# Graph attention on one core: two PSUM banks for the picked destinations, running maxima in SBUF, and another order in the drain

## The chip, the cores and the metric

One core of one Trainium2 chip runs the whole program. The metric is the time of one execution in microseconds (us), lower is better. TensorE (PE) does matmuls and transposes, VectorE (DVE) and ScalarE (ACT) work element by element, GpSimd (POOL) here does nothing but issue indirect DMAs (gathers and one scatter, by indices that lie in SBUF), and SyncE (SP) issues ordinary DMAs. PSUM has 8 banks of 128 x 512 f32.

## The reference

A graph has 12500 nodes with 128 features and 212500 edges, sorted by destination. For each edge three logits per head (8 heads of 16) are formed, each gets a softmax over the edges of one destination, and the sum of the three softmaxes weights the destination's value vector:

```python
h = relu(layernorm(x))
q = h @ Wq.T + bq;  k = edge_attr @ Wk.T + bk;  v = h @ Wv.T + bv
in_m   = sum(q[src] * k, per head)
out_m  = sum(q[dst] * k, per head)
diag_m = sum(q[src] * q[dst], per head)
score = (segment_softmax(in_m / 4, dst) + segment_softmax(out_m / 4, dst)
         + segment_softmax(diag_m / 4, dst)) * edge_weight ** lam
h = segment_sum(score * v[dst], dst)
out = x + leaky_relu(h @ Wo.T + bo, 0.1)
```

## The kernel before, in words

**Node pass.** `node_pass` normalises x and writes the tables q_tab (queries of all nodes) and v_tab to HBM. POOL meanwhile gathers 77 of 99 rows of destination numbers (`fetch_rows`, L141), which DVE compares and counts (`count`, L129 and L133) to find the last edge of each node.

**Edge pass.** `edge_pass` goes over 104 units of 16 tiles of 128 edges, each unit in 4 groups of 4 tiles. Per group: POOL gathers 4 tiles of source queries from q_tab (`fetch_sources`, L150, 16 gathers a unit, 1664 in all) into a ring `qsrc` of 8 groups; SP loads windows of q_tab around the group's destinations (L744); DVE makes a one-hot mask from the destination numbers (`pick_mask`, L1004); PE picks the destinations' queries by a matmul of window and mask into `qd_ps` (`pick`, L822), multiplies the edge features by Wk into `k_ps` (`keys`, L811) and transposes the gathered sources into `qs_ps` (`turn`, L831). ACT copies `qd_ps` and `k_ps` to `kq` (`take_qd` L897, `take_k` L891), DVE forms the three products (`products`, L1014 and L1018), and PE sums them over the heads into `lg_ps` (`sums_of_heads`, L802).

Per unit, one unit later: DVE scans the logits for running maxima per segment into `max_ps` (`running_max`, L1029), ACT copies them to `sums` (`take_max`, L909), DVE forms the differences (L1035, L1037, L1040), ACT takes their exponentials (`exps`, L913 to `terms`, and L914, the decay factors, over `max_ps`), and DVE weights the terms (`running_sums`, L1045) and scans twice for running sums (L1050). Two units later PE transposes maxima and sums into `t_ps` (`turn_sums`, L842), ACT copies them to `rows` (`take_rows`, L921), and `finish_unit` stores them to `state` in HBM (L931).

All orders are written out by hand in each engine's `unit(h, q)`; there is no scheduler. PE asks in `pick` that ACT has copied every earlier pick, since `qd_ps` is one bank:

```python
need(pe, qd_copied, n)
```

DVE calls `running_max` after the products of a unit's group 0, and `running_sums` after those of group 3, in the last unit ahead of those of group 3. ACT calls `exps` at group 2.

**Drain.** What follows POOL's last source gather is called the drain: the last logits, maxima and sums, their store, the join of the 128 partitions' ends (`join_ends`, `join_fix`), a gather of one row each of `state` (L777), its repaired version scattered back (L782), and the last destination rows (`fetch_rows` for blocks 7 and 8, 11 gathers each; block 7 stands ahead of the wait for the stores, `rows_out`, and block 8 between L777 and L782).

**Out pass.** POOL gathers 98 times 128 rows of `state` (`fetch_results`, L159), and the rest turns them into the output behind it.

Of the kernel before, what the change touches and what calls it, by code (L numbers as in the profile page):

```python
# [24 lines left out]
P = 128  # L25
# [19 lines left out]
A = 3  # L45
# [544 lines left out]
def edge_pass(nc, env):  # L590
# [8 lines left out]
    with ExitStack() as ctx:  # L599
# [14 lines left out]
        prod = sb("prod", [P, 2, A, GRP * P])  # L614
        terms = sb("terms", [P, 2, A, W1])
        sums = sb("sums", [P, 2, 3, A, W1])
        diffs = sb("diffs", [P, 2, A, W1])
# [25 lines left out]
        k_ps = psum("k_ps", [P, 2, GRP * P])  # L643
        qd_ps = psum("qd_ps", [P, GRP * P])
        qs_ps = psum("qs_ps", [P, 2, GRP * P])
        max_ps = psum("max_ps", [P, A, W1])
        lg_ps = psum("lg_ps", [P, A, W1])
# [111 lines left out]
        @block.gpsimd  # L759
        def _(pool):  # L760
            def unit(h, q):
                u = QUAD * h + q
                pool.wait_ge(idx_in[q], 16 * (h + 1))
                for g in range(NG):
                    need(pool, qs_turned, NG * u + g - RING + 1)
                    pool.sem_inc(pool_turns, 1)
                    fetch_sources(pool, q, g)

            for b in range(2):
                pool.wait_ge(env["q_out"][b], 16 * (NSTEP // 2))  # L770
            pool.wait_ge(env["zeros_out"], 16)
            over_units(pool, unit)

            fetch_rows(pool, NEARLY, tile_i)
            for b in range(2):
                pool.wait_ge(rows_out[b], 16 * (NCOL // 2))
            pool.indirect_dma_start(out=fix[:, :, :].rearrange("p k c -> p (k c)"), out_offset=None, in_=state,  # L777
                                    in_offset=bass.IndirectOffsetOnAxis(ap=fix_i[:, 0:1], axis=0)
                                    ).then_inc(fix_in, 16)
            fetch_rows(pool, NB - 1, tile_i)  # L780
            pool.wait_ge(fixed_ready, 1)
            pool.indirect_dma_start(out=state, out_offset=bass.IndirectOffsetOnAxis(ap=fix_i[:, 0:1], axis=0),  # L782
                                    in_=fixed[:, :, :].rearrange("p k c -> p (k c)"), in_offset=None
                                    ).then_inc(fix_out, 16)
            pool.wait_ge(edge_step, 20)
            pool.wait_ge(env["rows_used"], NEARLY)
            pool.wait_ge(fix_out, 16)
            pool.sem_inc(pool_turns, 1)
            for k in range(RST):
                fetch_results(pool, k)  # L790

        @block.tensor
        def _(pe):
# [20 lines left out]
            def pick(h, q, m):  # L814
                n = NG * (QUAD * h + q) + m
                r, w = slot(q, m)
                pe.wait_ge(window_in[r], 16 * GRP * (2 * h + w + 1))
                need(pe, qd_copied, n)
                pe.wait_ge(onehot_ready, n + 1)
                for j in range(GRP):  # L820
                    at = slice(j * P, (j + 1) * P)
                    t = nc.tensor.matmul(qd_ps[:, at], window[:, r, j, :], onehot[:, m % 2, at], start=True, stop=True)  # L822
                t.then_inc(qd_ready, 1)
# [22 lines left out]
            def unit(h, q):  # L846
                v = scanned(h, q)
                for g in range(NG):
                    if exists(h, q, g + 1):
                        pick(h, q, g + 1)  # L850
                        keys(h, q, g + 1)
                    if is_last(h, q) and g == NG - 1:
                        for k in range(3):
                            turn_sums(NCOL - 2, 0, k)
                    if exists(h, q, g - 1) and g != 1:
# [5 lines left out]
                    if g == 1:  # L861
                        sums_of_heads(h, q, g - 1)

            env["nodes_done"](pe)
# [3 lines left out]
            over_units(pe, unit)  # L868
            sums_of_heads(NQUAD, 0, -1)
            for k in range(3):  # L870
                turn_sums(NCOL - 1, 1, k)
# [5 lines left out]
            for k in range(2):  # L877
                t = nc.tensor.transpose(qd_ps[0:CH, k * P:(k + 1) * P], pens[:, k, :], ident[:, :])
            t.then_inc(ends_turned, 1)
# [6 lines left out]
        def _(act):  # L886
# [7 lines left out]
            def take_qd(h, q, m):  # L894
                n = NG * (QUAD * h + q) + m
                act.wait_ge(qd_ready, n + 1)
                nc.scalar.copy(kq[:, m % 2, 1, :], qd_ps[:, :]).then_inc(qd_copied, 1)  # L897

# [8 lines left out]
            def take_max(v, b):  # L907
                act.wait_ge(max_ready, v + 1)
                nc.scalar.copy(sums[:, b, 0, :, :], max_ps[:, :, :]).then_inc(max_copied, 1)  # L909

            def exps(v):
                act.wait_ge(diffs_ready, v + 1)
                nc.scalar.activation(terms[:, 0, :, 1:W1], diffs[:, 1, :, 1:W1], ACT.Exp, scale=SCALE)  # L913
                nc.scalar.activation(max_ps[:, :, :], diffs[:, 0, :, :], ACT.Exp, scale=SCALE).then_inc(exps_ready, 1)  # L914

# [29 lines left out]
            def unit(h, q):  # L945
                v = scanned(h, q)
                for g in range(NG):
# [12 lines left out]
                    if g == 2 and done:  # L960
                        finish_unit(v - 1, q % 2)
                    if g == 2 and v is not None:
                        exps(v)
                    if is_last(h, q) and g == NG - 1:
                        take_rows(NCOL - 2, 0, 0)
                        take_rows(NCOL - 2, 0, 1)
                        finish_unit(NCOL - 2, 0)

# [7 lines left out]
            over_units(act, unit)  # L976
            seed(NCOL - 1)
            take_max(NCOL - 1, 1)
            take_rows(NCOL - 1, 1, 0)
            exps(NCOL - 1)  # L980
# [11 lines left out]
        def _(dve):  # L992
# [29 lines left out]
            def running_max(v, p, n, b):  # L1022
# [5 lines left out]
                pen = pa_sb[:, p, 0:A, :]  # L1028
                nc.vector.tensor_tensor_scan(max_ps[:, :, :].rearrange("p a i -> p (a i)"),  # L1029
                                             pen.rearrange("p a i -> p (a i)"),  # L1030
# [5 lines left out]
                                        ).then_inc(logits_used, 1)  # L1036
                nc.vector.tensor_tensor(shifted[:, :, :], max_ps[:, :, 0:P],  # L1037
                                        pen[:, :, 1:W1], ALU.add).then_inc(shift_ready, 1)
                dve.wait_ge(shift_ready, v + 1)
                nc.vector.tensor_tensor(diffs[:, 0, :, 1:W1], shifted[:, :, :], max_ps[:, :, 1:W1], ALU.subtract  # L1040
                                        ).then_inc(diffs_ready, 1)

            def running_sums(v, p, b):
# [5 lines left out]
                for k in (1, 2):  # L1049
                    s = nc.vector.tensor_tensor_scan(sums[:, b, k, :, :].rearrange("p a i -> p (a i)"),  # L1050
                                                     max_ps[:, :, :].rearrange("p a i -> p (a i)"),
                                                     terms[:, k - 1, :, :].rearrange("p a i -> p (a i)"), 0.0,
# [3 lines left out]
            def unit(h, q):  # L1056
# [3 lines left out]
                for g in range(NG):  # L1060
                    if is_last(h, q) and g == 3:
                        running_sums(v, p, 1 - q % 2)
# [13 lines left out]
            def join_ends():  # L1076

                dve.wait_ge(ends_turned, 1)
                nc.vector.tensor_copy(ends[:, 0:3, :], k_ps[0:CH, 0, 0:3 * P].rearrange("p (k n) -> p k n", k=3))
                nc.vector.tensor_copy(ends[:, 3:5, :], qd_ps[0:CH, 0:2 * P].rearrange("p (k n) -> p k n", k=2)  # L1080
                                      ).then_inc(join_step, 1)
# [388 lines left out]
```

## Time and profile before

| | us |
|---|---|
| median of 3 runs | 2389.36 (2387.71 to 2393.61) |
| the profiled execution | 2390.79 |
| span of its records | 2389.0 |
| PE busy | 1799.0 (75%) |
| DVE busy | 1749.4 (73%) |
| ACT busy | 933.9 (39%) |
| POOL busy | 1775.7 (74%) |

The profiled execution's own time is 1.8 us above its span and 1.4 us above the median. Times within the trace count from the start of the span. An engine's busy time leaves out register, branch, semaphore and DMA-issuing instructions on the queues, but POOL's indirect DMAs are counted, since POOL works out their descriptors. An idle time is put down to what ended last before it ended; "issue" is idle time in which the engine waited for nothing that the profile shows.

### The profile page before, as it was taken

What the parts mean: (1) busy time and instruction counts of PE and PEld (TensorE: products, weight loads), DVE (VectorE), ACT (ScalarE), POOL (GpSimd) and SP (SyncE); (2) the same over time, 40 slices, a digit from 0 to 9 for tenths busy, and PEclk for the clock granted to TensorE, in tenths of its full rate; (3) what the DMA queues carried; (4) which work ended last, traced back from release to release, by engine and by line L of the source; (5) the groups of instructions that cost most, each with busy time, mean ns of one, the idle gap of its engine ahead of it and who ended that gap; (6) DMA issues with size and microseconds to landing.
All of it is one profiled execution on the core that took longest, in us unless ns stands there. A gap on an engine that the chain in (4) does not pass through costs nothing.

```text
span 2389.0 us, 44129 instructions
## 1 busy us (share of the span) xinstructions
PE 1799.0 (75%) x10768; PEld 1101.8 (46%) x10768; DVE 1749.4 (73%) x2904; ACT 933.9 (39%) x1931; POOL 1775.7 (74%) x1869
## 2 busy tenths in 40 slices
PE   5557888887778777777777777878878788877277
PEld 4424444444444444444444444444444444444155
DVE  6749887777777777777777777777777777777456
ACT  5413444443434444344344443443434334434112
POOL 5777777777777777777777777777777777777575
PEclk9868998888989889889898898898888888899567
DMA  7797887777777777777777777777777777774345
GB/s 259 227 297 217 247 260 230 224 224 221 231 229 225 218 233 227 231 219 222 224 233 223 231 220 221 233 222 223 232 220 233 224 224 229 226 218 123 125 146 169
DMA packets 440885, 527.91 MB, mean 221 GB/s; under 512 B 87325, under 2 KB 306721, under 8 KB 440850
## 3 DMA queue, kind: packets, MB, share of 16 engines
q1 hardware_dynamic: 297858, 227.38, 32.1%
q10 hardware_dynamic: 83376, 180.80, 21.7%
q0 software_dynamic: 59616, 119.35, 19.5%
q8 instruction: 12, 0.20, 0.0%
q14 instruction: 23, 0.19, 0.0%
HBM read 442.67 MB, written 84.57 MB: 221 GB/s over the span
## 4 chain that ended last, share of the span: by engine, by line
POOL 56%; issue 20%; PE 10%; DMA 6%; DVE 6%; ACT 1%; POOLq 1%; SPq 0%; ACTq 0%; DVEq 0%
POOL qsrc L150 52%; DMA qsrc<-q_tab,idx_sb 5%; POOL rows_i L159 4%; PE qd_ps L822 3%; PE k_ps L811 2%; PE lg_ps L802 1%; PE qs_ps L831 1%; PE qv_ps L397 1%; PE t_ps L842 1%; ACT hb L337 1%; DVE prod L1018 1%; POOLq L69 0%; POOL rows_i L141 0%; DMA pa_tab<-pa 0%; DMA window<-q_tab 0%
## 5 line engine op out<-in xcount | busy, mean ns | idle before, releaser
L150 POOL DMA_INDIRECT qsrc<-q_tab,idx_sb x1664 | 1581.9, 951 | 507.3 <-issue 497.5
L831 PE MATMUL qs_ps<-ident,qsrc 128*128 128x128 f32 x1664 | 297.9, 309 | 377.7 <-DMA qsrc<-q_tab,idx_sb 376.8
L822 PE MATMUL qd_ps<-onehot,window 128*128 128x128 f32 x3328 | 531.0, 311 | 65.8 <-DVE onehot L1004 57.6
L897 ACT COPY kq<-qd_ps 128x512 f32<-128x512 f32 x416 | 243.1, 584 | 845.7 <-PE qd_ps L822 838.6
L1018 DVE TENSOR_TENSOR prod<-qs_ps,kq 128x1024 f32<-128x1024 f32 x416 | 506.7, 1218 | 89.2 <-PE qs_ps L831 86.3
L822 PEld LDWEIGHTS qd_ps<-onehot,window 128*128 128x128 f32 x3328 | 479.6, 222 | 139.9 <-issue 79.1
L1014 DVE SCALAR_TENSOR_TENSOR prod<-k_ps,bk_col,kq 128x512 f32<-128x512 f32 x416 | 308.8, 742 | 300.8 <-PE lg_ps L802 278.7
L811 PE MATMUL k_ps<-ea_sb,wk_sb 128*128 128x512 f32 x832 | 497.9, 684 | 30.5 <-DMA ea_sb<-in_ea 30.5
L831 PEld LDWEIGHTS qs_ps<-ident,qsrc 128*128 128x128 f32 x1664 | 216.3, 159 | 467.9 <-issue 466.9
L802 PE MATMUL lg_ps<-prod,heads 128*32 128x384 f32 x3328 | 359.3, 504 | 0.0
L891 ACT ACTIVATE kq<-k_ps,bk_col 128x512 f32<-128x512 f32 x416 | 286.0, 688 | 181.6 <-PE k_ps L811 156.8
L1004 DVE TENSOR_SCALAR_CACHE_REDUCE onehot<-near_sb,node_col 128x512 f32<-128x512 bf16 x416 | 306.0, 736 | 4.4 <-DMA near_sb<-near_tab 4.4
L842 PEld LDWEIGHTS t_ps<-ident,sums 128*128 128x128 f32 x936 | 120.3, 156 | 232.9 <-issue 221.8
L1050 DVE TENSOR_TENSOR_SCAN sums<-max_ps,terms 128x387 f32<-128x387 f32 x208 | 189.0, 950 | 3.6
L802 PEld LDWEIGHTS lg_ps<-prod,heads 128*32 128x32 f32 x3328 | 66.3, 109 | 269.6 <-issue 173.2
L842 PE MATMUL t_ps<-ident,sums 128*128 128x128 f32 x936 | 181.6, 307 | 10.7 <-DVE sums L1050 7.3
L921 ACT COPY rows<-t_ps 128x384 f32<-128x384 f32 x312 | 149.4, 479 | 78.3 <-PE t_ps L842 66.8
L811 PEld LDWEIGHTS k_ps<-ea_sb,wk_sb 128*128 128x128 f32 x832 | 149.9, 225 | 30.8 <-issue 30.8
L1029 DVE TENSOR_TENSOR_SCAN max_ps<-pa_sb,lg_ps 128x387 f32<-128x387 f32 x104 | 100.3, 965 | 61.2 <-ACT terms L904 56.2
L141 POOL DMA_INDIRECT rows_i<-in_dst_rows,tile_i x99 | 98.8, 998 | 44.9 <-issue 29.9
L159 POOL DMA_INDIRECT rows_i<-state,last_i x98 | 92.7, 946 | 31.7 <-issue 29.6
L1035 DVE TENSOR_TENSOR diffs<-lg_ps,sums 128x384 f32<-128x384 f32 x104 | 58.1, 558 | 57.0 <-ACT sums L909 57.0
(147 smaller groups left out, 1013.5 us busy)
## 6 DMA issues: line engine op xcount, KB each, us to landing
ea_sb<-in_ea ACTq DMA_DIRECT2D x416, 256.0 KB
window<-q_tab SPq DMA_DIRECT2D x1664, 64.0 KB
state<-rows ACTq DMA_DIRECT2D x104, 576.0 KB
near_sb<-near_tab SPq DMA_DIRECT2D x104, 512.0 KB, 8.3
pa_sb<-pa_tab SPq DMA_DIRECT2D x104, 258.0 KB
qsrc<-q_tab,idx_sb POOLq DMA_INDIRECT x1664
xs<-in_x SPq DMA_DIRECT2D x27, 448.0 KB, 5.8
q_tab<-qs SPq DMA_DIRECT2D x14, 448.0 KB, 2.8
```

Source lines behind the costliest of these rows:

```text
L150: pool.indirect_dma_start(out=qsrc[:, r, j, :], out_offset=None, in_=q_tab, in_offset=bass.IndirectOffsetOnAxis(ap=idx_sb[:, q, g * GRP + ...
L802: t = nc.tensor.matmul(lg_ps[2 * SUP * j:2 * SUP * (j + 1), :, 1:W1], heads[:, g, :], prod[:, m % 2, :, j * P:(j + 1) * P], start=g == 0, ...
L811: nc.tensor.matmul(k_ps[:, m % 2, :], wk_sb[:, :], ea_sb[:, p, g * GRP * P:(g + 1) * GRP * P], start=True, stop=True).then_inc(k_ready, 1)
L822: t = nc.tensor.matmul(qd_ps[:, at], window[:, r, j, :], onehot[:, m % 2, at], start=True, stop=True)
L831: t = nc.tensor.transpose(qs_ps[:, m % 2, j * P:(j + 1) * P], qsrc[:, r, j, :], ident[:, :])
L842: t = nc.tensor.transpose(t_ps[:, a * P:(a + 1) * P], sums[:, b, k, a, 1:W1], ident[:, :])
L891: nc.scalar.activation(kq[:, m % 2, 0, :], k_ps[:, m % 2, :], ACT.Identity, bias=bk_col[:, 0:1]).then_inc(k_copied, 1)
L897: nc.scalar.copy(kq[:, m % 2, 1, :], qd_ps[:, :]).then_inc(qd_copied, 1)
L1004: nc.vector.tensor_scalar(onehot[:, m % 2, :].rearrange("p (j i) -> p j i", j=GRP), near_sb[:, p, :, :].rearrange("p (j g) i -> p g j i", ...
L1014: nc.vector.scalar_tensor_tensor(out=prod[:, g % 2, 2, :], in0=k_ps[:, g % 2, :], scalar=bk_col[:, 0:1], in1=kq[:, g % 2, 1, :], op0=ALU.a ...
L1018: nc.vector.tensor_tensor(prod[:, g % 2, 0:2, :], qs_ps[:, g % 2, :].unsqueeze(1).to_broadcast([P, 2, GRP * P]), kq[:, g % 2, :, :], ALU.m ...
L1050: s = nc.vector.tensor_tensor_scan(sums[:, b, k, :, :].rearrange("p a i -> p (a i)"), max_ps[:, :, :].rearrange("p a i -> p (a i)"), terms ...
```

## The change

`qd_ps` gets two banks, taken in turn, and PE's `pick` then waits for the pick before the last. To make room, the tile `max_ps` (PSUM, one bank) becomes `max_sb` in SBUF; everything that wrote or read the one now writes or reads the other. In the last unit, ACT takes the exponentials at group 1 and DVE scans the sums ahead of the products of group 2; PE and ACT spread the transposes and copies of unit 102 between those of the last unit. POOL fetches both last blocks of destination rows ahead of the wait for the stores. Lines after `max_sb`'s declaration stand one further down.

```diff
+        max_sb = sb("max_sb", [P, A, W1])
...
-        qd_ps = psum("qd_ps", [P, GRP * P])
+        qd_ps = psum("qd_ps", [P, 2, GRP * P])
         qs_ps = psum("qs_ps", [P, 2, GRP * P])
-        max_ps = psum("max_ps", [P, A, W1])
...
-            fetch_rows(pool, NEARLY, tile_i)
+            for m in range(NEARLY, NB):
+                fetch_rows(pool, m, tile_i)
             for b in range(2):
                 pool.wait_ge(rows_out[b], 16 * (NCOL // 2))
             pool.indirect_dma_start(out=fix[:, :, :].rearrange("p k c -> p (k c)"), out_offset=None, in_=state,
...
-            fetch_rows(pool, NB - 1, tile_i)
             pool.wait_ge(fixed_ready, 1)
...
-                need(pe, qd_copied, n)
+                need(pe, qd_copied, n - 1)
...
-                    t = nc.tensor.matmul(qd_ps[:, at], window[:, r, j, :], onehot[:, m % 2, at], start=True, stop=True)
+                    t = nc.tensor.matmul(qd_ps[:, m % 2, at], window[:, r, j, :], onehot[:, m % 2, at], start=True, stop=True)
...
-                    if is_last(h, q) and g == NG - 1:
-                        for k in range(3):
-                            turn_sums(NCOL - 2, 0, k)
...
+                    if is_last(h, q) and g == NG - 1:
+                        turn_sums(NCOL - 2, 0, 0)
...
             sums_of_heads(NQUAD, 0, -1)
+            for k in range(1, 3):
+                turn_sums(NCOL - 2, 0, k)
...
-                nc.scalar.copy(sums[:, b, 0, :, :], max_ps[:, :, :]).then_inc(max_copied, 1)
+                nc.scalar.copy(sums[:, b, 0, :, :], max_sb[:, :, :]).then_inc(max_copied, 1)
...
-                nc.scalar.activation(max_ps[:, :, :], diffs[:, 0, :, :], ACT.Exp, scale=SCALE).then_inc(exps_ready, 1)
+                nc.scalar.activation(max_sb[:, :, :], diffs[:, 0, :, :], ACT.Exp, scale=SCALE).then_inc(exps_ready, 1)
...
-                    if g == 2 and v is not None:
+                    if g == (1 if is_last(h, q) else 2) and v is not None:
                         exps(v)
                     if is_last(h, q) and g == NG - 1:
                         take_rows(NCOL - 2, 0, 0)
-                        take_rows(NCOL - 2, 0, 1)
-                        finish_unit(NCOL - 2, 0)
...
             seed(NCOL - 1)
+            take_rows(NCOL - 2, 0, 1)
             take_max(NCOL - 1, 1)
+            finish_unit(NCOL - 2, 0)
...
-                nc.vector.tensor_tensor(shifted[:, :, :], max_ps[:, :, 0:P],
+                nc.vector.tensor_tensor(shifted[:, :, :], max_sb[:, :, 0:P],
                                         pen[:, :, 1:W1], ALU.add).then_inc(shift_ready, 1)
...
-                nc.vector.tensor_tensor(diffs[:, 0, :, 1:W1], shifted[:, :, :], max_ps[:, :, 1:W1], ALU.subtract
+                nc.vector.tensor_tensor(diffs[:, 0, :, 1:W1], shifted[:, :, :], max_sb[:, :, 1:W1], ALU.subtract
...
-                                                     max_ps[:, :, :].rearrange("p a i -> p (a i)"),
+                                                     max_sb[:, :, :].rearrange("p a i -> p (a i)"),
                                                      terms[:, k - 1, :, :].rearrange("p a i -> p (a i)"), 0.0,
...
-                    if is_last(h, q) and g == 3:
+                    if is_last(h, q) and g == 2:
                         running_sums(v, p, 1 - q % 2)
```

How the order moves at the places where it matters. POOL from its last source gathers on, before (the number at a row's end is how many in a row):

```order
L150 DMA qsrc<-q_tab,idx_sb 128x128 x64
L141 DMA rows_i<-in_dst_rows,tile_i 128x128 x11
L777 DMA fix<-state,fix_i 128x72
L141 DMA rows_i<-in_dst_rows,tile_i 128x128 x11
L782 DMA state<-fixed,fix_i 212992x72
```

and after the change:

```order
L150 DMA qsrc<-q_tab,idx_sb 128x128 x64
L141 DMA rows_i<-in_dst_rows,tile_i 128x128 x22
L778 DMA fix<-state,fix_i 128x72
L782 DMA state<-fixed,fix_i 212992x72
L159 DMA rows_i<-state,last_i 128x72 x28
```

The 11 gathers of block 8 have moved from between the row gather and the scatter to before both. PE from the last transposes of sources to the join, before:

```order
L831 MATMUL qs_ps<-ident,qsrc 128x128 x4
L842 MATMUL t_ps<-ident,sums 128x128 x9
L802 MATMUL lg_ps<-prod,heads 32x3x128 x8
L842 MATMUL t_ps<-ident,sums 128x128 x9
```

and after the change:

```order
L831 MATMUL qs_ps<-ident,qsrc 128x128 x4
L802 MATMUL lg_ps<-prod,heads 32x3x128 x4
L842 MATMUL t_ps<-ident,sums 128x128 x3
L802 MATMUL lg_ps<-prod,heads 32x3x128 x4
L842 MATMUL t_ps<-ident,sums 128x128 x15
```

The last two head sums stand ahead of six of the nine transposes of unit 102. DVE per unit keeps its order, only the operands move; the running sums of a unit after the change (a scan is printed as SCALAR_TENSOR_TENSOR):

```order
L1046 TENSOR_TENSOR terms<-terms,pa_sb 128x3x128
L1051 SCALAR_TENSOR_TENSOR sums<-max_sb,terms 128x387 x2
L1015 SCALAR_TENSOR_TENSOR prod<-k_ps,bk_col,kq 128x512
```

where before they read

```order
L1045 TENSOR_TENSOR terms<-terms,pa_sb 128x3x128
L1050 SCALAR_TENSOR_TENSOR sums<-max_ps,terms 128x387 x2
L1014 SCALAR_TENSOR_TENSOR prod<-k_ps,bk_col,kq 128x512
```

Both scans now take both inputs from SBUF, as L1037 and L1040 (L1038 and L1041 after the change) do too.

## Rows read from the trace of the kernel before

**Rows 1.** The page's chain that ended last, by engine and by line.
```profile
POOL 56%; issue 20%; PE 10%; DMA 6%; DVE 6%; ACT 1%; POOLq 1%; SPq 0%; ACTq 0%; DVEq 0%
```
**Rows 2.** Line L150: its instructions, idle time before them, who waited for it.
```profile
L150 POOL DMA_INDIRECT qsrc<-q_tab,idx_sb x1664: 940/945/2622, 117.4 to 2205.3; - x185
  issue: 497.5, 1632
  PE qs_ps L831: 9.7, 32
...
  PE qs_ps L831: 376.8, 136
```
**Rows 3.** Timeline, POOL: start us, us, instruction, count, idle time before it.
```profile
1430.58 0.94 POOL L150 DMA_INDIRECT qsrc<-q_tab,idx_sb  x1 [0.30 <-issue]
1431.83 1.28 POOL L150 DMA_INDIRECT qsrc<-q_tab,idx_sb  x1 [0.30 <-issue]
1433.41 0.95 POOL L150 DMA_INDIRECT qsrc<-q_tab,idx_sb  x1 [0.31 <-issue]
...
1452.16 1.30 POOL L150 DMA_INDIRECT qsrc<-q_tab,idx_sb  x1 [0.30 <-issue]
...
119.88 2.62 POOL L150 DMA_INDIRECT qsrc<-q_tab,idx_sb  x1 [0.31 <-issue]
```
**Rows 4.** Timeline, DVE, at the same places.
```profile
1431.73 0.56 DVE L1045 TENSOR_TENSOR terms<-terms,pa_sb 128x384 f32<-128x384 f32 x1
1432.33 1.82 DVE L1050 TENSOR_TENSOR_SCAN sums<-max_ps,terms 128x387 f32<-128x387 f32 x2
...
1452.09 0.55 DVE L1045 TENSOR_TENSOR terms<-terms,pa_sb 128x384 f32<-128x384 f32 x1
...
119.79 1.89 DVE L572 TENSOR_TENSOR pa<-power,same 128x1664 f32<-128x1664 f32 x1
```
**Rows 5.** Timeline of all engines near 1018: DVE's L1040 and a POOL gather.
```profile
1018.56 0.55 DVE L1040 TENSOR_TENSOR diffs<-shifted,max_ps 128x384 f32<-128x384 f32 x1
1018.64 0.95 POOL L150 DMA_INDIRECT qsrc<-q_tab,idx_sb  x1 [0.30 <-issue]
```
**Rows 6.** Groups of instructions: busy us, mean ns of one, idle before.
```profile
L1050 DVE TENSOR_TENSOR_SCAN sums<-max_ps,terms 128x387 f32<-128x387 f32 x208 | 189.0, 950 | 3.6
L1045 DVE TENSOR_TENSOR terms<-terms,pa_sb 128x384 f32<-128x384 f32 x104 | 57.7, 555 | 4.5 <-ACT max_ps L914 4.5
L1040 DVE TENSOR_TENSOR diffs<-shifted,max_ps 128x384 f32<-128x384 f32 x104 | 57.6, 554 | 3.6
L1037 DVE TENSOR_TENSOR shifted<-max_ps,pa_sb 128x384 f32<-128x384 f32 x104 | 56.9, 547 | 0.0
L913 ACT ACTIVATE terms<-diffs 128x384 f32<-128x384 f32 x104 | 54.4, 523 | 46.8 <-issue 46.6 <-DVE diffs L1040 0.2
L914 ACT ACTIVATE max_ps<-diffs 128x387 f32<-128x387 f32 x104 | 49.8, 479 | 0.0
```
**Rows 7.** Timeline of POOL in the drain.
```profile
2206.56 0.95 POOL L141 DMA_INDIRECT rows_i<-in_dst_rows,tile_i  x1 [0.30 <-issue]
...
2232.15 0.94 POOL L777 DMA_INDIRECT fix<-state,fix_i  x1 [12.16 <-DMA state<-rows]
...
2247.14 0.98 POOL L782 DMA_INDIRECT state<-fixed,fix_i  x1 [0.30 <-issue]
2250.30 0.97 POOL L159 DMA_INDIRECT rows_i<-state,last_i  x1 [2.18 <-DMA state<-fixed,fix_i]
```
**Rows 8.** DMA issues: the gather of the row to repair, us to landing.
```profile
fix<-state,fix_i POOLq DMA_INDIRECT x1, 2.5
```
**Rows 9.** Timeline of the other engines in the drain.
```profile
2211.02 0.56 DVE L1045 TENSOR_TENSOR terms<-terms,pa_sb 128x384 f32<-128x384 f32 x1 [3.53 <-ACT max_ps L914]
...
2225.63 1.61 DVE L129 TENSOR_TENSOR le<-rows_i,nid 128x1408 f32<-128x1408 int32 x1
...
2240.31 0.18 DVE L1114 TENSOR_TENSOR best<-carry,fix 128x24 f32<-128x24 f32 x1
...
2241.70 0.20 DVE L1126 TENSOR_TENSOR fixed<-part 128x48 f32<-128x48 f32 x1
```

More of the change, by code:

```diff
@@ L877, in _ @@
             for k in range(2):
-                t = nc.tensor.transpose(qd_ps[0:CH, k * P:(k + 1) * P], pens[:, k, :], ident[:, :])
+                t = nc.tensor.transpose(qd_ps[0:CH, 0, k * P:(k + 1) * P], pens[:, k, :], ident[:, :])
             t.then_inc(ends_turned, 1)
@@ L896, in take_qd @@
                 act.wait_ge(qd_ready, n + 1)
-                nc.scalar.copy(kq[:, m % 2, 1, :], qd_ps[:, :]).then_inc(qd_copied, 1)
+                nc.scalar.copy(kq[:, m % 2, 1, :], qd_ps[:, m % 2, :]).then_inc(qd_copied, 1)
             def seed(v):
@@ L1028, in running_max @@
                 pen = pa_sb[:, p, 0:A, :]
-                nc.vector.tensor_tensor_scan(max_ps[:, :, :].rearrange("p a i -> p (a i)"),
+                nc.vector.tensor_tensor_scan(max_sb[:, :, :].rearrange("p a i -> p (a i)"),
                                              pen.rearrange("p a i -> p (a i)"),
@@ L1079, in join_ends @@
                 nc.vector.tensor_copy(ends[:, 0:3, :], k_ps[0:CH, 0, 0:3 * P].rearrange("p (k n) -> p k n", k=3))
-                nc.vector.tensor_copy(ends[:, 3:5, :], qd_ps[0:CH, 0:2 * P].rearrange("p (k n) -> p k n", k=2)
+                nc.vector.tensor_copy(ends[:, 3:5, :], qd_ps[0:CH, 0, 0:2 * P].rearrange("p (k n) -> p k n", k=2)
                                       ).then_inc(join_step, 1)
```

## The prediction

> **What bounds the kernel now.** I read the chain that ended last first: POOL with its "issue" gaps makes up 76% of it [rows 1]. Then the line that POOL spends it on, L150: 1664 gathers, the first at 117.4 us and the last at 2205.3, so 1.2555 us from one to the next (2087.9 / 1663). Of that 0.945 is the median instruction and 0.30 the gap behind it, 1.25 together [rows 2, 3]. A unit's 16 gathers take 20.0 us, and nothing else sets the pace: POOL's waits for PE are 32 of 0.30 us each (9.7 in all), which is no more than the ordinary gap, while PE waits 376.8 us for gathered sources [rows 2]. So in this stage of 2089 us PE, ACT and DVE have some 3.6 us of slack per unit (376.8 / 104), and whatever lengthens POOL's gathers lengthens the kernel one for one.
>
> What does lengthen them? The reader should put POOL's long instructions beside DVE's. The gather at 1431.83 takes 1.28 us instead of 0.945. It started 0.10 us into DVE's L1045, which ends at 1432.29; 0.335 late means that it was held until 1432.17. The one at 1452.16 was held by 0.355, until 1452.52, and L1045 ended at 1452.64. The longest gather of all, at 119.88, was held by 1.675, until 121.56, with L572 from 119.79 to 121.68 [rows 3, 4]. All three are held until 0.12 us before the end of a DVE instruction that was already running when they started, and both instructions read **two tensors from SBUF**. The gather at 1433.41 starts inside the scans L1050, which read one tensor from PSUM and one from SBUF, and takes 0.95; the one at 1018.64 starts inside L1040, PSUM and SBUF too, and takes 0.95 [rows 3, 4, 5]. So it is not DVE's activity that holds POOL, but its two SBUF inputs, and a gather is held only if it starts while such an instruction runs.
>
> **The two banks for the picks.** They let PE pick a group ahead. The work that hides this is POOL's pace: PE waits for sources anyway. Priced at 0; with the cover gone (POOL faster) it could only gain. Nothing is queued behind a new wait here, one is loosened.
>
> **The exponentials and copies on ACT.** L914 now writes SBUF. The nearest row is L913, to SBUF: 523 ns for 384 elements against 479 for 387 to PSUM [rows 6]. 0.04 us, 104 times, is 4.6 us on an engine that is 39% busy, hidden by the same slack; 0. The ScalarE copy of the maxima reads SBUF instead; the same slack hides it. The Trainium skill, "ScalarE: Activation LUTs" (Step-by-step: what each stage is for), says that PSUM is the lower-latency destination for ScalarE; were these 4.6 us on the path, the sum would be 4.6 higher, and here they are not.
>
> **The operands on DVE.** This is the term that decides. Per unit, before, one instruction with two SBUF inputs, L1045, 0.555 us, holds for 0.43 (0.12 less). With gathers every 1.25 us at a phase that drifts, the mean hold is 0.43 x 0.43 / 2 / 1.25 = 0.074 us a unit, 7.7 us over 104. The trace bears this out: 1581.9 busy (1664 x 0.951, the page) less 1664 x 0.945 is 9.4, of which 1.7 is the one at 119.88. After the change, five such instructions:
> - L1037 and L1040, 0.55 each [rows 6], in one cluster: 2 x 0.074 = 0.148 a unit.
> - L1045 with both scans behind it, 0.95 each, 1.82 together [rows 4, 6]. From the start of L1045 they hold over 0 to 0.43, 0.59 to 1.42 and 1.46 to 2.29. The first gather of the cluster starts at s, evenly over 1.25. For s under 0.43 (34%) it is held 0.215 on average, starts its successor at 1.68 and that is held until 2.29, 0.61: 0.83 together. For s from 0.43 to 0.59 (13%) only the successor is held, 0.53. For s above (53%) it is held 0.50 on average by the first scan, and its successor comes after everything. Mean: 0.34 x 0.83 + 0.13 x 0.53 + 0.53 x 0.50 = 0.616.
>
> So 0.616 + 0.148 - 0.074 = 0.69 us a unit more, and over the 102 units whose sums fall in POOL's stage **+70.4 us**. That a scan with two SBUF inputs holds as a plain TENSOR_TENSOR does is not in the trace: no such scan of full width runs beside a gather. Its bounds are 0, by the scans with one PSUM input (0.95, not held), which leaves the 0.148 alone, +15.1 us; and, if POOL does not get in between two scans 0.04 us apart, hold until the second one's end, 1.37 instead of 0.50: 1.076 + 0.148 - 0.074 = 1.15 a unit, +117.3. I take the middle, because the scan's two reads are what L1045 does, and because every held gather got in 0.12 before the holder's end. In the other direction nothing in the rows lets DVE be faster by it.
>
> The Trainium skill, "SBUF — State Buffer" (Who interferes with whom), says that a DVE instruction with two SBUF inputs contends with a GpSimd instruction that reads SBUF; by that alone the sum is as above. But the same section infers that `tensor_tensor` takes only the read side and that descriptor generation, which needs the write side, goes on beside it; by that the sum would be the drain's gain alone, 2381. The trace has a gather held by 1.675 us beside a TENSOR_TENSOR [rows 3, 4], so I weigh it low.
>
> **The drain.** Before: POOL does 11 gathers from 2206.56, waits for the last store until 2232.15 (12.16 us idle), gathers the row, does 11 more, scatters at 2247.14 and starts the results at 2250.30, 3.2 later [rows 7]. After: 22 gathers from 2206.56, 27.5 us, end at 2234.1. The last store has landed by 2232 in any case, so the row's gather goes out at 2234.1 and lands 2.5 later [rows 8], at 2236.6. DVE's join needs 1.6 us from there (2240.31 to 2241.9) if the carries are there [rows 9]. They were at 2240.3, 8.2 after the store landed. The new order must bring them 3.7 us forward: in the last unit DVE waited 3.53 us idle for the exponentials and then did 2.4 us of sums before the last products [rows 9]; with the sums earlier the last logits, and everything behind them, come some 5 us sooner. So the scatter goes out at 2238.3 instead of 2247.14: **-8.8 us**, or -5.1 if the reordering brings nothing (carries at 2240.3, scatter at 2242). The 98 result gathers and the end behind them only shift. Against it: two more clusters beside these gathers (1.4), and the comparison L129, two SBUF inputs and 1.61 us, which ran while POOL waited [rows 9] and now meets its gathers, 1.49 x 1.49 / 2 / 1.25 = 0.9: +2.3.
>
> **The sum** is 70.4 + 2.3 - 8.8 = +63.9 on the profiled 2390.79, 2454.7. The median stands 1.4 below that execution, so I say **2453**.
>
> **The rivals.**
> - *POOL cannot get in between two scans.* +117.3 + 3.2 - 8.8 = +111.7: 2501. For it: they are only 0.04 us apart by the hold's end. Against: nothing observed. 15%.
> - *Scans do not hold POOL.* Then 15.1 + 1.2 - 8.8 = +7.5: 2397. For it: no row shows one. Against: they read the same two sides. 15%.
> - *Faster.* POOL's holds are peculiar to the operand `pa_sb` and to L572, not to two SBUF inputs, and none is added: the drain alone is left, -8.8: 2381. It decides from where the added holds stay under 8.8 us, 0.085 a unit. Against: L1037 reads `pa_sb` already, and the longest hold is by L572, which reads neither; 6% covers both. The page's inference on the write side would give the same time.
> - *PE is the bound and the second bank helps.* It would need POOL waiting for PE; its 32 waits are 0.30 each [rows 2]. Under 2%.
>
> **How the numbers follow.** 62% for the forecast, whose own range is 2433 to 2473: a quarter of the holds either way, since phases need not be even. The range that holds the time 8 times in 10 takes in the rivals of 15% on both sides, 2395 to 2505. A measurement of this kernel can tell 0.3%, 7 us, from no change. Faster by more: the 6%, less what falls within: 0.05. Within: half of the scans' rival and some of the last: 0.09. Slower: 0.86.
>
> **What would show it.** The gathers of L150 in the profile after: median still 0.945, but mean near 0.993, with the long ones starting inside the two scans (some 100 of them, up to 0.83 longer), L1037 and L1040; the pace 1.298 us a gather; the last L150 near 2276. Holds of up to 1.7 us would show that POOL does not get in between. Gathers of 0.945 inside the scans would prove me wrong, as would waits of POOL for PE of more than 0.3. In the drain, no idle time of POOL before the row's gather, and some 8 us less from the last L150 to the first L159. PE's wait for sources should grow.

## The result, and the profile after

The changed kernel takes 2443.34 us (median of 5 runs, 2439.45 to 2448.48) against 2389.4 for the kernel before (5 runs): a ratio of 1.0225, 95% interval 1.0213 to 1.0238. It is slower by 54 us, where 64 were forecast. The profiled execution has a span of 2441.5 us, 52.5 more than before.

The page's chain that ended last is still POOL's, more so than before [rows 1]:

```profile
POOL 62%; issue 21%; DMA 7%; PE 6%; DVE 3%; POOLq 1%; ACT 1%; ACTq 0%; SPq 0%; DVEq 0%
```

Line L150, which answers to [rows 2] (durations in ns min/median/max, then the first and last start):

```profile
L150 POOL DMA_INDIRECT qsrc<-q_tab,idx_sb x1664: 940/944/2640, 118.1 to 2265.1; - x185
  issue: 498.2, 1634
  PE qs_ps L831: 9.1, 30
...
  PE qs_ps L831: 390.3, 152
```

Median and idle time are what they were; the stage from the first to the last L150 has grown from 2087.9 to 2147.0 us, by 59.1. The page's group of that line says where: the gathers themselves are longer, 1640.9 us busy where there were 1581.9.

```profile
L150 POOL DMA_INDIRECT qsrc<-q_tab,idx_sb x1664 | 1640.9, 986 | 507.3 <-issue 498.2
```

The timeline of POOL shows which ones; columns as in [rows 3]:

```profile
643.69 1.22 POOL L150 DMA_INDIRECT qsrc<-q_tab,idx_sb  x1 [0.30 <-issue]
645.21 1.49 POOL L150 DMA_INDIRECT qsrc<-q_tab,idx_sb  x1 [0.30 <-issue]
...
661.99 0.94 POOL L150 DMA_INDIRECT qsrc<-q_tab,idx_sb  x1 [0.30 <-issue]
663.23 1.64 POOL L150 DMA_INDIRECT qsrc<-q_tab,idx_sb  x1 [0.30 <-issue]
665.18 0.94 POOL L150 DMA_INDIRECT qsrc<-q_tab,idx_sb  x1 [0.30 <-issue]
```

and DVE's timeline at the same places, which answers to [rows 4]:

```profile
643.54 0.56 DVE L1046 TENSOR_TENSOR terms<-terms,pa_sb 128x384 f32<-128x384 f32 x1
644.13 1.82 DVE L1051 TENSOR_TENSOR_SCAN sums<-max_sb,terms 128x387 f32<-128x387 f32 x2
...
663.16 1.82 DVE L1051 TENSOR_TENSOR_SCAN sums<-max_sb,terms 128x387 f32<-128x387 f32 x2
```

The gather at 663.23 starts 0.07 into the first scan and is held by 0.70 us, that is, takes 1.64 where an undisturbed one takes 0.94. The one at 643.69 starts in the weighting and is held by 0.28; its successor then starts 1.08 after the scans' start, in the second one, and is held by 0.55. This is the cluster of the forecast. In the whole stage 52 gathers are held by the first scan and 51 by the second, always until 0.77 to 0.78 and 1.62 to 1.64 us from the scans' start, 46.9 us together; plain TENSOR_TENSORs let go 0.11 to 0.13 before their end, as before. Not every gather that starts under such an instruction is held: of those that started before the point where it lets go, 193 were held, and the 8 that started in its first 0.03 us were not.

In the drain POOL's rows, which answer to [rows 7], read

```profile
2265.09 0.94 POOL L150 DMA_INDIRECT qsrc<-q_tab,idx_sb  x1 [0.30 <-issue]
2266.34 0.94 POOL L141 DMA_INDIRECT rows_i<-in_dst_rows,tile_i  x1 [0.30 <-issue]
...
2295.10 0.94 POOL L778 DMA_INDIRECT fix<-state,fix_i  x1 [0.30 <-issue]
2299.47 2.11 POOL L782 DMA_INDIRECT state<-fixed,fix_i  x1 [3.43 <-DVE fixed L1127]
2304.11 0.97 POOL L159 DMA_INDIRECT rows_i<-state,last_i  x1 [2.53 <-DVE edge_f L1152]
```

POOL has no idle time ahead of the row's gather any more, and from the last L150 to the first L159 it is 39.0 us instead of 45.0. The scatter itself takes 2.11: DVE's timeline shows the comparison of the last block starting 0.36 before it.

```profile
2298.99 0.20 DVE L1127 TENSOR_TENSOR fixed<-part 128x48 f32<-128x48 f32 x1
2299.11 1.62 DVE L129 TENSOR_TENSOR le<-rows_i,nid 128x1408 f32<-128x1408 int32 x1
```

The bill against before: start of the stage +0.7 (118.1 for 117.4), stage +59.1, drain -6.0, from the first L159 to the end of the span -1.3 (137.4 for 138.7): +52.5.

### The profile page after: what moved, and what is told of

Its sections match the earlier page's. It is cut to its first block, busy times and chain, and to the rows that moved or that the text cites. A ratio compares the mean times of both kernels' runs of the same rounds, so it can differ in the third digit from the quotient of the medians.

```text
span 2441.5 us, 44129 instructions
## 1 busy us (share of the span) xinstructions
PE 1798.3 (74%) x10768; PEld 1086.0 (44%) x10768; DVE 1749.5 (72%) x2904; ACT 933.9 (38%) x1931; POOL 1838.3 (75%) x1869
## 4 chain that ended last, share of the span: by engine, by line
POOL 62%; issue 21%; DMA 7%; PE 6%; DVE 3%; POOLq 1%; ACT 1%; ACTq 0%; SPq 0%; DVEq 0%
POOL qsrc L150 58%; DMA qsrc<-q_tab,idx_sb 5%; POOL rows_i L159 4%; PE qd_ps L822 1%; PE qs_ps L831 1%; PE k_ps L811 1%; PE qv_ps L397 1%; POOL rows_i L141 1%; ACT hb L337 1%; DMA pa_tab<-pa 0%; POOLq L69 0%; PE t_ps L842 0%; PE lg_ps L802 0%; DVE stats L473 0%; DMA window<-q_tab 0%
## 5 line engine op out<-in xcount | busy, mean ns | idle before, releaser
L150 POOL DMA_INDIRECT qsrc<-q_tab,idx_sb x1664 | 1640.9, 986 | 507.3 <-issue 498.2
L831 PE MATMUL qs_ps<-ident,qsrc 128*128 128x128 f32 x1664 | 290.6, 303 | 391.0 <-DMA qsrc<-q_tab,idx_sb 390.3
L831 PEld LDWEIGHTS qs_ps<-ident,qsrc 128*128 128x128 f32 x1664 | 209.1, 155 | 484.1 <-issue 481.3
L802 PE MATMUL lg_ps<-prod,heads 128*32 128x384 f32 x3328 | 367.2, 514 | 0.1
L842 PEld LDWEIGHTS t_ps<-ident,sums 128*128 128x128 f32 x936 | 114.3, 150 | 220.7 <-issue 215.4
L1030 DVE TENSOR_TENSOR_SCAN max_sb<-pa_sb,lg_ps 128x387 f32<-128x387 f32 x104 | 99.6, 958 | 141.5 <-ACT terms L905 119.0
L1051 DVE TENSOR_TENSOR_SCAN sums<-max_sb,terms 128x387 f32<-128x387 f32 x208 | 189.3, 952 | 3.6
L842 PE MATMUL t_ps<-ident,sums 128*128 128x128 f32 x936 | 174.8, 298 | 6.2 <-DVE sums L1051 4.1
L159 POOL DMA_INDIRECT rows_i<-state,last_i x98 | 92.9, 948 | 32.1 <-issue 29.6
```

Of the source, the lines that this page charges most:

```text
L150: pool.indirect_dma_start(out=qsrc[:, r, j, :], out_offset=None, in_=q_tab, in_offset=bass.IndirectOffsetOnAxis(ap=idx_sb[:, q, g * GRP + ...
L159: pool.indirect_dma_start(out=st[:, k % RST, j, :], out_offset=None, in_=state, in_offset=bass.IndirectOffsetOnAxis(ap=last_i[:, at:at + 1 ...
L802: t = nc.tensor.matmul(lg_ps[2 * SUP * j:2 * SUP * (j + 1), :, 1:W1], heads[:, g, :], prod[:, m % 2, :, j * P:(j + 1) * P], start=g == 0, ...
L831: t = nc.tensor.transpose(qs_ps[:, m % 2, j * P:(j + 1) * P], qsrc[:, r, j, :], ident[:, :])
L842: t = nc.tensor.transpose(t_ps[:, a * P:(a + 1) * P], sums[:, b, k, a, 1:W1], ident[:, :])
```

## The experiments

**Which part costs.** Everything of the kernel before but the tile of the maxima:

```diff
-        max_ps = psum("max_ps", [P, A, W1])
+        max_sb = sb("max_sb", [P, A, W1])
```

(and its name wherever it is used).

> The kernel before with the maxima and decay factors in SBUF and nothing else of the change (one bank for the picks, the old drain). Theory (POOL's gathers are held by DVE instructions with two SBUF inputs): L150 takes about 1640 us busy instead of 1581.9, its pace is some 1.29 us a gather, and the kernel some 60 us slower than before, 2450, so slower than the changed kernel by the drain's 6 to 7 us. Rival A (the second bank or PE's new order changed the pace): L150 stays near 1582 and the kernel near 2390. Rival B (something in the drain costs the time): 2390 too.

Measured: 2448.1 us (2445.47 to 2452.09) beside a kernel before of 2391.42, ratio 1.024 (1.0221 to 1.0258); from the last L150 to the first L159 43.1 us. Its group of L150:

```profile
L150 POOL DMA_INDIRECT qsrc<-q_tab,idx_sb x1664 | 1642.4, 987 | 507.6 <-issue 496.9 <-PE qs_ps L831 10.7
```

The loss is all in the move to SBUF; rivals A and B fall.

**Maxima in SBUF, decay factors in PSUM.** One bank for the picks leaves a bank for the decay factors:

```diff
-        max_ps = psum("max_ps", [P, A, W1])
+        decay = psum("decay_ps", [P, A, W1])
+        max_sb = sb("max_sb", [P, A, W1])
...
-                nc.scalar.activation(max_ps[:, :, :], diffs[:, 0, :, :], ACT.Exp, scale=SCALE).then_inc(exps_ready, 1)
+                nc.scalar.activation(decay[:, :, :], diffs[:, 0, :, :], ACT.Exp, scale=SCALE).then_inc(exps_ready, 1)
...
-                                                     max_ps[:, :, :].rearrange("p a i -> p (a i)"),
+                                                     decay[:, :, :].rearrange("p a i -> p (a i)"),
```

> One bank for the picks; the running maxima lie in SBUF, but the decay factors get the PSUM bank, so L1037 and L1040 have two SBUF inputs and the scans of the sums still have one. Theory: only 2 x 0.074 us per unit is added, L150 near 1597 us busy (+15), kernel near 2404, no gather held inside the scans. Rival C (it is the maxima's tile in SBUF, written by a scan and read by ACT, that costs, whatever the second scans read): most of the 59 us stays, near 2440.

Measured: 2405.38 us (2402.76 to 2406.18), ratio 1.0059 (1.0042 to 1.0076), and

```profile
L150 POOL DMA_INDIRECT qsrc<-q_tab,idx_sb x1664 | 1596.3, 959 | 507.6 <-issue 498.5 <-PE qs_ps L832 9.2
```

14.4 us more than before in L150, where 15 were expected. The same scans, now with decay factors from PSUM, do not hold POOL: 141 gathers start inside them and none is held. The two subtractions hold 55 gathers, by 11.7 us together.

**The converse.** Maxima in PSUM, decay factors in SBUF:

```diff
+        decay = sb("decay_sb", [P, A, W1])
```

with the same two uses as above.

> One bank for the picks; the maxima stay in PSUM, the decay factors lie in SBUF, so the two scans of the sums have two SBUF inputs and L1037 and L1040 keep one. Theory: the scans' holds alone, up to 0.77 us each: L150 near 1630 us busy (+45 to +50), kernel near 2436. Rival C would give 2390. The two parts should add up: what this and the run with the maxima in SBUF lose together is what both in SBUF lose.

Measured: 2440.22 us (2438.84 to 2442.06), ratio 1.0211 (1.0194 to 1.0228), and

```profile
L150 POOL DMA_INDIRECT qsrc<-q_tab,idx_sb x1664 | 1628.5, 979 | 507.3 <-issue 496.6 <-PE qs_ps L832 10.4 <-DMA idx_sb<-in_idx 0.3
```

+46.6. The two parts give 14.4 + 46.6 = 61.0; together in one kernel they gave 60.5 (the first experiment) and 59.0 (the change). DVE executes the same instructions on the same elements in all of these kernels and only the memory of an operand differs, so it is the second SBUF input that holds POOL: rival C falls. ScalarE's reads and writes change memory in these kernels too, but the held gathers come free at a fixed time from the start of a DVE instruction, 0.77 us for the first scan in this run as well.

**The second bank.** The changed kernel with one bank:

```diff
-        qd_ps = psum("qd_ps", [P, 2, GRP * P])
+        qd_ps = psum("qd_ps", [P, GRP * P])
...
-                need(pe, qd_copied, n - 1)
+                need(pe, qd_copied, n)
```

> The changed kernel with one bank for the picks again and the wait for the pick before. Theory: the second bank is worth nothing under POOL's pace, so the same time as the changed kernel within 0.3%, 2443, and the same 1641 us busy in L150. Rival D (the second bank gives back part of what the holds cost): slower than the changed kernel, by 10 us or more.

Measured: 2444.66 us (2438.95 to 2449.72), ratio to before 1.0219 (1.02 to 1.0238); the changed kernel's was 1.0225 (1.0213 to 1.0238). L150 1644.2 us busy. The second bank, for which the PSUM was cleared, brings nothing that can be measured here.

**The drain alone.** The kernel before with both blocks fetched ahead and the last unit's new order (all of the change's diff but the banks and the tile):

> The kernel before with the new drain alone (both blocks of rows ahead, the last unit's new order); maxima in PSUM, one bank. Theory: no added holds in the stage of L150 (busy near 1582), from the last L150 to the first L159 about 37 to 38 us instead of 45.0, kernel near 2382. Rival (the new order delays the stage before it): 2389 or more.

Measured: 2384.5 us (2380.51 to 2390.13, 9 runs) against 2390.6, ratio 0.9975 (0.9965 to 0.9986). L150 1582.6 busy; 38.6 us from the last L150 to the first L159. The scatter is held by DVE's comparison here too:

```profile
2236.15 0.94 POOL L778 DMA_INDIRECT fix<-state,fix_i  x1 [0.30 <-issue]
2240.53 2.11 POOL L782 DMA_INDIRECT state<-fixed,fix_i  x1 [3.44 <-DVE fixed L1127]
2245.47 0.96 POOL L159 DMA_INDIRECT rows_i<-state,last_i  x1 [2.83 <-DVE edge_f L1157]
```

with DVE's

```profile
2240.17 1.62 DVE L129 TENSOR_TENSOR le<-rows_i,nid 128x1408 f32<-128x1408 int32 x1
```

**Its two halves.** Only the fetch:

```diff
-            fetch_rows(pool, NEARLY, tile_i)
+            for m in range(NEARLY, NB):
+                fetch_rows(pool, m, tile_i)
...
-            fetch_rows(pool, NB - 1, tile_i)
```

> Only the fetch of the last block of rows is moved ahead, the order of the last unit is the old one. Theory: the carries come at the old time, so the scatter waits for DVE: 5 us less from the last L150 to the first L159, near 40, kernel near 2384. Rival (the order of the last unit brings nothing, POOL's 22 gathers set the time alone): the same as with both, 37 to 38.

Measured: 2386.86 us (2384.24 to 2391.38), ratio 0.9988 (0.9979 to 0.9997); 41.5 us from the last L150 to the first L159. POOL waits 6.76 us for DVE's join ahead of the scatter, so the order of the last unit is needed for the rest:

```profile
2241.76 2.11 POOL L782 DMA_INDIRECT state<-fixed,fix_i  x1 [6.76 <-DVE fixed L1126]
```

Only the order of the last unit (the edits of `unit` on PE, ACT and DVE, as in the change's diff):

> Only the order of the last unit is new, the last block of rows is fetched between the row's gather and the scatter as before. Theory: the last store leaves 5 us earlier, POOL waits 7 us instead of 12.16 for it and everything behind moves by 5: near 40 from the last L150 to the first L159, kernel near 2384. Rival (PE's and ACT's new order delays as much as it brings): 45, 2389.

Measured: 2385.47 us (2381.09 to 2389.38), ratio 0.9979 (0.997 to 0.9988); 38.3 us from the last L150 to the first L159, better than expected. The row's gather comes after 5.14 us of idle time instead of 12.16, and the 11 gathers behind it keep the scatter out of the comparison's way:

```profile
2225.28 0.94 POOL L777 DMA_INDIRECT fix<-state,fix_i  x1 [5.14 <-DVE cnt L133]
2240.25 0.98 POOL L782 DMA_INDIRECT state<-fixed,fix_i  x1 [0.30 <-issue]
```

So the order alone brings 6.7 of those 45.0 us and the fetch alone 3.5, but both only 6.4: with all 22 gathers ahead POOL reaches the row's gather late, waits 3.44 for DVE, and is held in the scatter.

**The gathers spread.** The drain alone, with the last block's 11 gathers in parts of 5, 4 and 2 (`fetch_rows` gets the range of its gathers as a new argument):

```diff
-            for m in range(NEARLY, NB):
-                fetch_rows(pool, m, tile_i)
+            fetch_rows(pool, NEARLY, tile_i)
+            fetch_rows(pool, NB - 1, tile_i, range(0, 5))
...
+            fetch_rows(pool, NB - 1, tile_i, range(5, 9))
             pool.wait_ge(fixed_ready, 1)
...
+            fetch_rows(pool, NB - 1, tile_i, range(9, LB))
```

> As with the new drain alone, but the 11 gathers of the last block are spread: 5 ahead of the wait for the stores, 4 between the row's gather and the scatter, 2 behind the scatter, where POOL otherwise waits 2.2 to 3.2 us for it to land. Theory: the scatter leaves 1 to 2 us earlier than with all 22 ahead and the wait behind it is filled, so 1 to 3 us less than with the new drain alone: 34 to 36 from the last L150 to the first L159, kernel near 2379. Rival (the gathers behind the scatter delay its landing or the last block's rows delay the out pass): no gain over the new drain alone.

Measured: 2380.86 us (2378.77 to 2385.88), ratio to before 0.996 (0.9947 to 0.9974); 34.3 us from the last L150 to the first L159:

```profile
2229.58 0.95 POOL L778 DMA_INDIRECT fix<-state,fix_i  x1 [0.30 <-issue]
...
2237.13 0.98 POOL L783 DMA_INDIRECT state<-fixed,fix_i  x1 [1.61 <-DVE fixed L1129]
2238.41 0.97 POOL L141 DMA_INDIRECT rows_i<-in_dst_rows,tile_i  x1 [0.30 <-issue]
2239.68 0.95 POOL L141 DMA_INDIRECT rows_i<-in_dst_rows,tile_i  x1 [0.30 <-DMA state<-fixed,fix_i]
2240.93 0.94 POOL L159 DMA_INDIRECT rows_i<-state,last_i  x1 [0.30 <-issue]
```

The scatter is not held, and the wait for its landing is filled. This version has the lowest median here, 9.7 us under the kernel before and 62 under the changed one; the interval of its ratio overlaps that of the drain alone. Its profiled execution, the longest of its five (2385.88 us), gains 10.7 in the drain but has 143.1 us from the first L159 to the end instead of 138.7. The same last part takes 142.6 in the one-bank kernel and 137.4 in the changed one, whose code there is the same, so such a difference need not come from the spreading.

**Holds in pieces.** If a gather is held only by the one instruction that runs when it starts, short instructions hold disproportionately little. In the changed kernel each scan, the weighting and the two subtractions become three instructions (the scans are shown, the others are cut in the same way):

```diff
-                    s = nc.vector.tensor_tensor_scan(sums[:, b, k, :, :].rearrange("p a i -> p (a i)"),
-                                                     max_sb[:, :, :].rearrange("p a i -> p (a i)"),
-                                                     terms[:, k - 1, :, :].rearrange("p a i -> p (a i)"), 0.0,
-                                                     ALU.mult, ALU.add)
+                    for a in range(A):
+                        s = nc.vector.tensor_tensor_scan(sums[:, b, k, a, :], max_sb[:, a, :], terms[:, k - 1, a, :],
+                                                         0.0, ALU.mult, ALU.add)
```

> The changed kernel with each of its DVE instructions that have two SBUF inputs (both scans of the sums, the weighting, both subtractions of the maxima) cut into three, one per kind of logit; the same elements and the same results. Theory (a gather is held only until the end of the one instruction that runs when it starts, and gets in between two): the mean hold goes with the square of an instruction's length, so with holds of some 0.22 us per piece of scan and 0.17 per piece of the others the unit loses 6 x 0.019 + 9 x 0.011 = 0.21 us instead of 0.62, which gives back about 42 us: L150 near 1598 busy, kernel near 2400, though DVE does more. Rival E (what holds POOL is how long DVE has two-SBUF work in a unit, in whatever pieces): no gain, 2443 or more, and gathers held over several pieces.

Measured: 3101.81 us, beside a kernel before of 3068.37 (3044.08 to 3089.68) on the same chip. All the runs from here on were taken on a chip on which the kernel before itself takes some 3070 us, so their times stand beside those alone, and POOL's pace was not the bound there. POOL is missing from the chain that ended last, and the group of L150 has 1083.6 us of idle time instead of 507.3:

```profile
another core or an unknown queue 28%; PE 24%; DVE 21%; issue 18%; ACT 5%; ACTq 2%; DMA 1%; SPq 0%; DVEq 0%
...
L150 POOL DMA_INDIRECT qsrc<-q_tab,idx_sb x1664 | 1592.2, 957 | 1083.6 <-issue 471.1 <-remote 270.7 <-PE qs_ps L831 185.5
```

What it does tell is how single gathers are held. Those that started inside pieces of the scans were held by at most 0.19 us each and 11.8 together, and the held ones came free 0.19 before the end of that piece, though the next piece followed at once; uncut, the scans held gathers by up to 0.72 and 46.9 together. So rival E's holds over several pieces are not there. L150 is 1592.2 us busy, 48.7 less than the changed kernel's 1640.9, where 1598 was expected, but the changed kernel itself was never run on this chip, so that difference also holds whatever POOL's longer waits change in how gathers meet DVE's instructions. The ratio to before is 1.0112 (1.007 to 1.0154); what makes it slower there stays open.

> The changed kernel with its DVE instructions of two SBUF inputs in thirds once more, since its first run was beside a kernel before of 3068 us, in which POOL waited for DMAs and PE and its pace did not set the time. Its records there already had L150 at 1592.2 us busy, where 1598 was expected. Theory: where the kernel before takes 2390 us, POOL's pace sets the time, L150 is again near 1595 busy, and the kernel takes some 2398: 45 us less than the changed kernel, and 8 more than the kernel before (14 more in the holds, 6 less in the drain). Rival E: 2443 or more. If the kernel before is again near 3070, only L150's busy time tells.

Measured, again on that chip: 3111.53 us beside 3070.55 (1.0149, 1.0091 to 1.0206), L150 1598.1 us busy, no gather held by more than 0.19 us inside a piece of a scan. That a gather is held by one piece alone and gets in before the next is confirmed in both runs; the gain in the time of the kernel (some 45 us were expected where POOL sets the pace) stays unmeasured.

**Pieces on the best version.** The weighting in three and the comparison L129 in four, on top of the spread drain:

> Maxima in PSUM and one bank as in the kernel before, the new drain with its last gathers spread, and the weighting L1045 cut into three and the comparison of the counts L129 into four pieces. Theory: of the 5 us that the weighting cost POOL 2 to 3 come back, of the 4.7 us that the comparisons cost some 3, so 5 us less than with the spread drain alone: kernel near 2376. Rival E: no change from 2381.

Measured: 3088.05 us beside 3068.37 (ratio 1.0076, 1.0046 to 1.0106), so it was not faster here. L153, its line of the source gathers, is 1580.3 us busy against 1584.5 for L150 with the spread drain alone. That difference proves little, since the kernels with the same DVE instructions in this stage (before, the drain alone, its two halves, the spread drain) lie between 1580.8 and 1584.5. The single gathers say more: the pieces of the weighting held 17 by at most 0.13 us, 1.1 together, where the whole one held 35 by 7.0. The destination rows' gathers are 93.8 us busy against 99.5, but that is not the pieces' doing: with the comparison whole they take 93.5 and 93.8 on this chip too (the two runs of the changed kernel in pieces).

> The same, and the four long comparisons and products of the node pass that have two SBUF inputs cut into four pieces each. Theory: in the kernel before they held four gathers by 5.1 us together (the longest by 1.68); in pieces by 1 to 2, so 3 to 4 us less again: near 2372. Rival: the node pass grows on DVE and PE starts later, so POOL's ring fills and it waits: no gain.

Measured: 3084.43 us beside 3068.37 (1.0055, 1.0024 to 1.0087); the source gathers 1577.8 us busy, 2.5 less again, of 3 to 4 expected, and within the spread just named. Whether either beats the spread drain where POOL is the bound is open.

## Why the prediction was right, point by point

- **POOL's pace bounds the stage, and nothing else does.** Right: with 59 us more in the gathers the stage is 59.1 longer, and POOL's waits for PE stayed 0.3 each (9.1 us in 30). The second bank at 0: right, by the experiment with one bank. ACT's exponentials to SBUF now take 509 ns instead of 479, 0.03 us more where the row gave 0.04, and DVE waits for them 1.2 us in all instead of 4.5. The rule of the Trainium skill ("ScalarE: Activation LUTs", Step-by-step: what each stage is for) that PSUM is the lower-latency destination agrees in direction; it states no size.
- **Two SBUF inputs hold POOL.** Right, and by experiment rather than by timing alone, since the same scans hold or do not hold with the memory of one operand. That scans hold as TENSOR_TENSORs do was the assumption with the least behind it, and it held. The rule of the Trainium skill ("SBUF — State Buffer", Who interferes with whom) that two SBUF inputs contend with a GpSimd instruction that reads SBUF agrees with this; its inference that descriptor generation goes on beside a `tensor_tensor` does not: of the gathers that started under one with two SBUF inputs in the changed kernel only those in its first 0.03 us and its last 0.13 went on unheld.
- **POOL gets in between two scans.** Right for the scans: releases at 0.77 and 1.63 us, no hold over both; the rival at 2501 falls. That holds go with the square of the length, which the sum rests on, agrees with the pieces: 11.8 us over 104 units are 0.11 a unit, as expected of the scans' six pieces (6 x 0.019), though on a chip where POOL also waits more.
- **The term of +70.4 was mis-sized.** It measured +59.1, and +60.5 and +62.3 in busy time in the two other kernels with everything in SBUF. The step that was off is the length of the scans' holds: taken as 0.83 each (0.12 off the 0.95), they are 0.77 and 0.75, since a scan lets go 0.19 before its end. With holds over 0 to 0.43, 0.59 to 1.36 and 1.46 to 2.22 the same working gives 0.34 x 0.75 + 0.13 x 0.46 + 0.53 x 0.44 = 0.55 instead of 0.616, so 0.55 + 0.148 - 0.074 = 0.62 a unit and 64 us. The 2 to 5 us left lie in the phases, which no run varied: the two subtractions held 56 gathers by 10.9 us together where an even phase makes it 15.1, and the weighting 31 by 6.3 where it makes 35 and 7.5.
- **The drain at -8.8 + 2.3 = -6.5.** It measured -6.0 between the same two rows. The step of the carries was right: they came 28.7 us after the last L150 (2293.8) instead of 35.0, more than the 3.7 needed, and the row landed 2.5 after its gather. What the prediction did not have is the hold of the scatter itself by L129, 1.17 us; the other holds there came to 1.3 of the 2.3 allowed, and the two errors nearly cancel.
- The sum, +63.9, against +52.5 in the span and 54 between the medians: the sign, the mechanism and the range hold, the size is 18% too large between medians.

## What to carry to other kernels

When GpSimd issues the DMAs that set a kernel's pace, look at its longest instructions beside DVE's: here the DVE instructions with two SBUF inputs delayed nearly every gather that started under them, so moving one tile from PSUM to SBUF cost 57 us (the first experiment) through an engine that the edit never named. Before clearing a PSUM bank for double buffering, read who waits: the engine that got the second bank was waiting for DMAs. Where one operand must lie in SBUF, choose the one that short instructions read (the maxima cost 14 us in the gathers, the decay factors 47).

## What had not been expected of the hardware

A scan lets POOL go 0.19 us before its end, a TENSOR_TENSOR 0.13. The scatter, whose indices (`fix_i`) lie in SBUF like the gathers', is held the same way (2.11 us instead of 0.98), so one comparison placed just ahead of it undid 1.2 us of a 9 us gain.

Two SBUF inputs are not the only thing that holds. The node pass of the kernel before has this on POOL and on DVE:

```profile
109.72 0.94 POOL L141 DMA_INDIRECT rows_i<-in_dst_rows,tile_i  x1 [0.30 <-issue]
110.97 2.53 POOL L141 DMA_INDIRECT rows_i<-in_dst_rows,tile_i  x1 [0.30 <-issue]
113.81 1.46 POOL L141 DMA_INDIRECT rows_i<-in_dst_rows,tile_i  x1 [0.30 <-issue]
...
108.70 1.89 DVE L512 TENSOR_SCALAR pa<-same 128x1664 f32<-128x1664 f32 x1
110.50 1.88 DVE L513 TENSOR_TENSOR near<-dst_i 128x1664 bf16<-128x1664 int32 x1
112.30 1.08 DVE L518 TENSOR_SCALAR same<-dist_sb,lam 128x1664 f32<-128x1664 f32 x1
113.42 1.03 DVE L521 TENSOR_SCALAR dist_sb<-dist_sb 128x1664 f32<-128x1664 f32 x1
```

L521 reads one tensor from SBUF, yet the gather at 113.81 is held by 0.51, until 0.13 before L521's end; in five of the later runs a source gather met this instruction and was held by 0.51 too. L512, which also reads one but takes 1.89 us for the same 1664 elements, holds nothing (the gather at 109.72). And POOL does not always get in between two instructions: the gather at 110.97 is held by 1.58, until 112.56, past the end of L513 and 0.26 into L518. Both stay open.

One chip ran the kernel before in some 3070 us instead of 2390. On it POOL's median gather took the same 0.94 to 0.95 in every kernel, the time going into its waits (1083.6 us idle at L150 in the changed kernel with pieces, 507.3 in the changed kernel elsewhere), and TensorE's mean granted clock was 0.80 to 0.82 where it was 0.85 to 0.88 elsewhere; what was slow there stays open.
